# Grouped attention: queries made turned with the weights stationary, and another order of the last slot's quads

## The reference

```
DIM, HEADS, KV_HEADS, HD = 1024, 32, 8, 32
q = (layernorm(x) @ Wq), 32 heads of 32     # per batch 112 x 1024
k = ctx @ Wk ; v = ctx @ Wv                 # 375 x 256, 8 heads
attn = softmax(q k^T / sqrt(32))            # 112 x 375 per head
x = x + tanh(g_xattn[2]) * (attn v) @ Wo
```

## Time and profile before

| | |
|---|---|
| median of 3 runs | 3226.4 us (3213.05 to 3229.02) |
| the profiled execution | 3231.93 us, span 3230.3 us |
| busy: PE, PEld | 2800.1 us (87%), 1972.8 us (61%) |
| busy: DVE, ACT, POOL | 2008.1 us, 1186.7 us, 452.8 us |
| mean granted PE clock | 0.929 of full speed |
| the grouped stage | about 1578 to 2323 us of the span |

### The profile page before, as it was taken

One profiled execution on the slowest core, in us unless ns is written; L12 is line 12 of the kernel. 1 busy time (PEld: TensorE's weight loads), 2 busy tenths in 40 slices (PEclk: granted clock), 3 DMA queues, 4 the chain that ended last, 5 costly groups with the idle time before them and its releaser, 6 DMA issues. The chain is left out here.

```text
span 3230.3 us, 54176 instructions
## 1 busy us (share of the span) xinstructions
PE 2800.1 (87%) x20468; PEld 1972.8 (61%) x20468; DVE 2008.1 (62%) x3515; ACT 1186.7 (37%) x2604; POOL 452.8 (14%) x516
## 2 busy tenths in 40 slices
PE   7999999999994699978689999999578898847888
PEld 4665665665662588856355655655377777635664
DVE  5545545545535776654567777775457887846774
ACT  2333333333332233312245555554255545311222
POOL 0110110110112100000012222222122322200000
PEclk9999999999997799986789999999699998967999
DMA  6100100100105545544433333331230001045441
GB/s 240 45 33 12 44 33 12 44 33 11 39 1 197 156 128 146 134 100 171 142 125 135 117 121 135 129 111 64 70 136 24 19 19 30 13 115 182 163 146 47
DMA packets 103179, 292.18 MB, mean 90 GB/s; under 512 B 33480, under 2 KB 56680, under 8 KB 93456
## 3 DMA queue, kind: packets, MB, share of 16 engines
q1 hardware_dynamic: 75408, 220.09, 20.3%
q0 software_dynamic: 18704, 53.14, 5.6%
q10 hardware_dynamic: 8848, 16.10, 1.9%
HBM read 246.24 MB, written 43.04 MB: 90 GB/s over the span
## 5 line engine op out<-in xcount | busy, mean ns | idle before, releaser
L1462 DVE TENSOR_REDUCE latent_nmax<-bank 112x1 f32<-112x487 f32 x128 | 85.2, 665 | 274.4 <-PE bank L1327 266.9
L1846 POOL TENSOR_SCALAR grouped_probs<-grouped_probs,grouped_rsum 112x375 f32<-112x375 f32 x256 | 152.7, 616 | 721.7 <-DVE grouped_rsum L1900 721.7
L2092 PE MATMUL bank<-ffn_qT,ffn_wgu 128*128 128x112 bf16 x4096 | 219.9, 219 | 22.6 <-ACTq L2163 13.3
L2092 PEld LDWEIGHTS bank<-ffn_qT,ffn_wgu 128*128 128x128 fp8e4 x4096 | 217.0, 102 | 27.4 <-issue 25.0
L1288 PEld LDWEIGHTS bank<-latent_hT,latent_wq 128*128 128x128 f32 x1536 | 182.1, 197 | 10.7 <-issue 10.2
L2231 POOL TENSOR_TENSOR ffn_h<-ffn_sl,ffn_us 128x448 f32<-128x448 f32 x64 | 135.4, 2116 | 360.1 <-ACTq L2186 360.1
L1251 POOL TENSOR_SCALAR latent_probs<-latent_probs,latent_rsum 112x487 f32<-112x487 f32 x128 | 88.0, 687 | 665.2 <-DVE latent_rsum L1467 665.2
L1288 PE MATMUL bank<-latent_hT,latent_wq 128*128 128x112 f32 x1536 | 181.0, 279 | 0.0
L1896 DVE TENSOR_REDUCE grouped_nmax<-bank 112x1 f32<-112x375 f32 x256 | 122.4, 541 | 92.5 <-PE bank L1723 89.8
L1810 ACT ACTIVATE grouped_probs<-bank,grouped_nmax 112x375 f32<-112x375 f32 x256 | 143.3, 572 | 75.7 <-DVE grouped_nmax L1896 75.7
L1266 PE MATMUL bank<-latent_wv,latent_hT 128*125 128x384 f32 (+1 forms) x512 | 167.8, 489 | 0.0
(11 more groups left out here) (398 smaller groups left out, 5808.0 us busy)
## 6 DMA issues: line engine op xcount, KB each, us to landing
grouped_raw<-L_weights SPq DMA_DIRECT2D x24, 2048.0 KB, 8.1
points_spread<-numbers SPq DMA_DIRECT2D x32, 912.0 KB
codes<-grouped_code SPq DMA_DIRECT2D x24, 512.0 KB, 6.0
latent_hT<-ctxT SPq DMA_DIRECT2D x8, 1500.0 KB, 6.9
plain_ctxT<-ctxT POOLq DMA_DIRECT2D x8, 1500.0 KB, 17.9
plain_ctx<-ctx POOLq DMA_DIRECT2D x8, 1500.0 KB, 35.1
grouped_ctx<-ctxT SPq DMA_DIRECT2D x8, 1500.0 KB, 12.2
latent_xy<-planes SPq DMA_DIRECT2D x8, 1024.0 KB, 8.5
```

Of the source, the lines that this page charges most:

```text
L1846: pool.tensor_scalar(pr[:, g % 2, j, :], pr[:, g % 2, j, :], rsum[:, g % 2, j:j + 1], 1.0, ALU.mult, ALU.mult)\
L2092: mm = pe.matmul(ahead.tile(t)[:, i * Q:(i + 1) * Q], wgu[:, u0 + f // 4, c:c + P], qT[:, k, :], start=(k == 0), stop=(k == KC - 1))
```

## The change

1. The queries come out turned. The weights are now the stationary side, 128 columns of `wq` at a time, and the 112 columns of `zT` move. Four groups of 8 matmuls fill one bank, 112 columns each; ACT copies a bank with the scale straight into `qT`. The item `qT`, its transposes, its two copies, its bank turns and the semaphore `q_ready` go. SP waits for the turned `z` before it loads the next one.
2. For g from `ALONE` = 59 on, PE does `scored(g)` behind tiles 0 and 1 of g-1; ACT does `last_tile(g-1)` ahead of `exponents(g)`; DVE does `tiles(g-1)` ahead of `maxima(g)`.

```diff
+    ALONE = N - QUADS + 3
...
-            ([("v0", 0, 8)], ["qT"], ["w8", ("v1", 0, 4)], [("v1", 4, 8), "o"]),
+            ([("v0", 0, 8)], [], ["w8", ("v1", 0, 4)], [("v1", 4, 8), "o"]),
...
             def normal(n):
                 if n >= 1:
-                    sp.wait_ge(turns.full(("qT", n - 1, 1)), turns.count(("qT", n - 1, 1), 0))
+                    sp.wait_ge(turns.full(("zT", n - 1, 1)), turns.count(("zT", n - 1, 1), 0))
                 sp.dma_start(z[:], x_in[n]).then_inc(z_loaded, 16)
...
                     elif kind == "q":
                         pe.wait_ge(zT_ready, n + 1)
-                        chunks(t, item, lambda k: zT[:, k, :], lambda k: wq[:, k, i * 512:(i + 1) * 512], Q, 512)
-                    elif kind == "qT":
-                        pe.wait_ge(q_ready, n + 1)
-                        turn_rows(pe, C, turns, q, "qT", n, 0)
+                        if item[1] == 0:
+                            pe.wait_ge(turns.free(t), turns.count(t, 0))
+                        for c in range(item[1], item[2]):
+                            m = c // 2
+                            for k in range(c % 2 * 4, c % 2 * 4 + 4):
+                                mm = pe.matmul(turns.tile(t)[:, m * Q:(m + 1) * Q], wq[:, k, (4 * i + m) * P:(4 * i + m + 1) * P], zT[:, k, :],
+                                               start=(k == 0), stop=(k == KC - 1))
+                        if item[2] == KC:
+                            mm.then_inc(turns.full(t), 1)
...
                 first, middle, ahead, last = PLAN[g % QUADS]
-                if 0 <= g < N:
+                if 0 <= g < ALONE:
                     scored(g)
                 do(first, g)
                 if 0 <= g - 1 < N:
                     turned(g - 1, 0)
                     turned(g - 1, 1)
+                if ALONE <= g < N:
+                    scored(g)
                 do(middle, g)
...
                     elif kind == "q":
-                        empty(t, q[:, i * 512:(i + 1) * 512], turns.tile(t)[0:Q, :], scale=SCALE)
+                        empty(t, qT[:, n % 2, 4 * i:4 * i + 4, :], turns.tile(t)[:, 0:4 * Q].rearrange("p (m q) -> p m q", m=4), scale=SCALE)
                         if i == 1:
-                            act.drain().then_inc(q_ready, 1)
-                    elif kind == "qT":
-                        copy_turned(act, turns, qT[:, n % 2], "qT", n, 0, qT_ready)
+                            act.drain().then_inc(qT_ready, 1)
...
+                if ALONE <= g <= N:
+                    last_tile(g - 1)
                 if 0 <= g < N:
                     exponents(g)
...
-                if 0 <= g - 1 < N:
+                if 0 <= g - 1 < ALONE - 1:
                     last_tile(g - 1)
...
+                if ALONE <= g <= N:
+                    tiles(g - 1)
                 if 0 <= g < N:
                     maxima(g)
...
-                if 0 <= g - 1 < N:
+                if 0 <= g - 1 < ALONE - 1:
                     tiles(g - 1)
```

More of the change, by code:

```diff
@@ L1514, in grouped_attention @@
         x, z = s_.sb("x", [Q, 2, D]), s_.sb("z", [Q, D])
-        q = z
         zT, qT, oT = s_.sb("zT", [P, KC, Q]), s_.sb("qT", [P, 2, KC, Q]), s_.sb("oT", [P, 2, KC, Q])
@@ L1535, in grouped_attention @@
         z_loaded = s_.sem("z_loaded")
-        z_ready, zT_ready, k_ready, v_ready, q_ready, qT_ready = (
-            s_.sem(n) for n in ("z_ready", "zT_ready", "k_ready", "v_ready", "q_ready", "qT_ready"))
+        z_ready, zT_ready, k_ready, v_ready, qT_ready = (
+            s_.sem(n) for n in ("z_ready", "zT_ready", "k_ready", "v_ready", "qT_ready"))
         max_ready, exp_ready, sum_ready, probs_ready, pT_ready, last_ready, oT_ready, x_done = (
@@ L1553, in at @@
                 return None
-            return (name, n, 0) if name in ("zT", "qT") else (name[0], n, int(name[1]))
+            return (name, n, 0) if name == "zT" else (name[0], n, int(name[1]))
         def bank(t, g):
@@ L1577, in uses @@
                         order.extend([(("zT", t[1], i), 4 + 2 * i) for i in range(2)])
-                    elif t[0] == "qT":
-                        order.extend([(("qT", t[1], i), 6 + i) for i in range(2)])
                     elif t[0] == "o":
```

## The result

| | before | changed |
|---|---|---|
| median | 3225.62 us (3212.28 to 3244.55, 20 runs) | 3240.83 us (3229.53 to 3254.4, 20 runs) |
| ratio, 95% interval | | 1.0045 [1.003, 1.006] |
| profiled execution | 3231.93 us, span 3230.3 | 3246.9 us, span 3245.3 |

The change costs 14.5 us by the ratio (9.7 to 19.4). The median lies inside the 0.5% that the forecast called "the same" (up to 3242.5), but only just; the kernel is a little slower, and that can be told only because there are 20 runs of each. The forecast was 3233.3 with a range of 3214 to 3251.

A forecast was written before the change was run, and what follows sets the result against it. PE bounds mid-stage; in the last batch's quads a chain through four engines does, mostly at the lower clock. Terms 2.8 - 1.7 + 5.8 = +6.9 us on the 3226.4 us median give 3233.3 us, range 3214 to 3251.

The forecast's parts named there:

- A: Query matmuls in the other orientation: four times as many weight loads, 0.35 us more a batch, +2.8 us in all.
- C: Last slots, quads 59 to 63: GpSimd enters the closed loop, turns of 10.1 us at the lower clock, +5.8 us.
- R2: Rival, steady batches: slot 6's longer hole drops the clock, about 2.5 us in each of 7 batches; 3250.8 us, chance 0.13.
- B: Query transposes and copies removed: nothing won in steady batches, 1.71 us in the prologue; -1.7 us in all.
- I take +2.8, the form's own undisturbed row: Query matmuls priced by the latent stage's same form, 0.1115 us an instruction, 14.27 us a batch.
- Cover and hole are the same: Slot 6: removed transposes lay inside PE's wait for DVE; hole grows from 0.95 to about 1.88 us, 7 batches give 0.
- turning before the scores is 8 x 0.21 = 1.68: Last slots, lower clock: the 8 transposes ahead of the scores take 1.68 us of the 10.1 us turn.
- the half turn at full clock: Last slots: 1.1 us taken off, half of one turn's difference (10.1 - 7.9), because the clock had once recovered before.
- R1: Rival: PE faster through cheaper queries, some steady transposes off the path, last slots at 2.4 GHz; 3216.5 us, chance 0.16.
- R3: Rival: the last slots' loop stays as long as before; +1.1 us in all, 3227.5 us, chance 0.15.
- R4: Rival: query weight loads do not hide beside matmuls, 0.29 us an instruction, +184 us, 3410 us, chance 0.01.

The follow-up runs named there:

- e1: The changed kernel with the last slots in the order of before, so only the queries part: 3228.72 us (12 runs), ratio 1.0005 [0.9982, 1.0027].
- e7: The changed kernel with query matmuls moving 56 columns instead of 112, every weight load kept: 3259.96 us (one run).
- e3: The kernel before without the second transposing of the queries and its copies; ACT copies unturned banks into qT: 3224.06 us (one run).
- e4: The changed kernel with 14 throw-away matmuls behind the output of each quad from 59 on: 3223.59 us (one run).
- e9: The changed kernel run once more, without an edit: 3238.87 us (8 runs), ratio 1.0047 [1.0025, 1.0068].
- e2: The kernel before with only the order of the last slots changed: 3236.9 us (12 runs), ratio 1.0017 [0.9991, 1.0043].
- e5: The kernel before with DVE's copies of tiles 0 and 1 ahead of the next quad's sums from quad 59 on: 3218.78 us (10 runs), ratio 0.9987.
- e8: The kernel before with 10 throw-away matmuls between second and third tile of each quad from 59 on: 3212.76 us (10 runs), ratio 0.9959 [0.9936, 0.9982].

## Why the prediction was right, point by point

The sign, the class and the main mechanisms held; A and C were too small, and R2's mechanism, which was given no place in the sum, came in one batch of seven. By the trace of the stage the terms stand at A +4.2 (predicted +2.8), B -1.4 (-1.7) and C +8.4 (+5.8). To them come three differences that no term had, mostly of the clock: +1.5 in slot 6 of batch 0, -2.3 in its first slots and -1.0 in slots 0 to 2 of batch 7. They take 1.8 off, so that +9.4 stands nearer to +6.9 than A and C do by themselves: that part is luck. By the runs the change costs 14.5 us, twice the forecast; the time stays within the range, which reached up to 3251 for the sake of R2. (The range does not quite follow from its text: R2 with 3 us added is 3253.8.)

- **A, queries: right in kind, small by a third.** Predicted 0.1115 us an instruction and +0.35 a batch; measured by the same two slots 0.1133 and +0.58 (2 x 7.25 against 2 x 6.96), and as whole batches +3.1 in the six steady ones (e1 +3.2). The step that was short is "I take +2.8, the form's own undisturbed row": groups of 16 do go at that row's pace (1.79 us, 0.112 each), but the 32 that follow the scores take 3.67 us, 0.115 each, near the upper end that the text gave (0.1148). e7 adds what the trace of before could not show: the moving columns don't set the pace. By the Trainium skill's rule for a load (TensorE: Matmul & The Clock Gate, section LDWEIGHTS), 107 ns for 128 columns, the pace would be just under the 112 ns that e7 shows with half the columns, and it would have made A a gain, which it is not.
- **B, second transposing: confirmed.** "Cover and hole are the same" holds: the hole is 1.71, predicted 1.88, w8 is where it was, and e3 shows it with that one part alone. The prologue gave -1.9 in e3, predicted -1.7; in the changed kernel -0.85, since its own dearer queries (+0.55) and a longer wait for ACT (+0.3) stand there too.
- **C, last slots: right in mechanism, +8.4 instead of +5.8.** GpSimd in the loop, 3.6 to 4.2 us of idle PE in front of each turning, a clock of 0.50, and 10.37 us a turn against the 10.1 of the sum. The link that was short is "turning before the scores is 8 x 0.21 = 1.68": from the turning to the scores it takes 2276.90 - 2274.95 = 1.95; why it is longer, no run shows. The other links came out within 0.05 us. Four times these 0.27, and 0.4 in the first turn at full clock (8.29 for 7.9), make 1.5. The other 1.1 is the half turn at full clock that the prediction took off; no turn of the changed kernel but the first ran at it.
- **R1, faster by the PE: refuted** in each of its three parts (A above the sum, no gain from B in steady batches, a clock of 0.57 in the last slots).
- **R2, clock falling behind the hole of slot 6: refuted for six batches of seven, true in one.** In the six steady batches the clock is 1.00 with a hole of 1.71 us in each slot 6. In batch 0 it fell behind a hole of the same length and cost 1.5 us (priced at 2.5), and the same in e1, e4 and e9. So a hole of that length can be followed by the lower clock; what sets batch 0 apart, no run shows.
- **R3, last slots not slower: refuted** by the trace of e2, +8.2 in the stage with that part alone.
- **R4, loads that don't hide: refuted**, 0.113 us an instruction and not 0.29. The rule cited for it (Trainium skill, same page, section The mechanism) is not borne out by e7 either, where load and matmul share all row groups and half the columns left the pace at 0.112. The same section also names a background buffer for weights as a way for a load to go ahead, which the prediction leaves out.
- **Left open:** about 5 us between the trace's +9.4 (+9.9 with what stands behind the stage) and the runs' +14.5. The intervals allow that there is nothing there, and no stage of the profiles shows it.

## What to carry to other kernels

Removing instructions from the busiest engine is worth what its next wait leaves of it: look for the hole behind them first (here 0.95 us released by DVE, and eight transposes a batch were worth nothing). The longer hole that they leave is not always free: in one batch of seven the clock fell behind it. Swapping the stationary and the moving side changes what is paid for, from columns moved to columns loaded; 128 loads of 128 columns here cost more than 32 runs of 512 columns. Where a pipeline runs out of cover, a step that was one quad behind is the slack of the slowest engine in it; an order that uses its result at once puts that engine, here 2.3 us of GpSimd and its handoffs, into every turn.

## What the runs showed of the hardware that was not expected

- **Throw-away matmuls make the kernel faster.** In the chain of the last slots the granted clock stood mostly at 0.50 (0.59 in the mean); 10 extra matmuls in each hole kept it at 1.00, took a turn from 8.05 or 8.53 to 6.77 us, and the whole to 0.9959 [0.9936, 0.9982]. In the changed kernel they took 2.1 us off a turn.
- **The clock can fall while the PE has work without a hole, and stay down.** In e7's prologue, behind a hole of 1.39 us that the changed kernel has too, the PE had work without a hole from 1607.56, where the queries start, to 1633.86, where the values do. The first 32 matmuls of 56 columns ran partly at full clock (4.14 us), and from 1612.56 on all were at the lower one: 64 instructions in 13.64 us, 0.213 each, where the steady ones take 0.112. The same program with 112 columns kept 1.00 there. This is one profile of e7. In e5 a PE busy 27.18 of 33 us stayed at 0.50 too, where e8 with 26.74 of 33 was at 1.00. Busy share alone does not tell the clock.
- **56 columns cost nearly what 112 do** behind a load of 128 columns: 0.112 and 0.115 us.
- **The clock fell behind a hole of 1.71 us in one batch of seven**, the same one in four profiles, and stayed at 1.00 behind the other six. In e7, with half the columns, it stayed at 1.00 behind a hole of 1.75 us in that batch too.
